# Turning two query tiles of each attention head by VectorE and DRAM instead of one, with every engine's order written for eight units

## What is computed

```python
h = jnp.maximum(_layernorm(x, axis=-1), 0.0)
# layer 2, and layer 3 in the same way with its own weights and biases
q, k, v = split_heads(h @ w_qkv)                       # 8 heads x 1024 x 32
attn = jnp.einsum('bhnd,bhmd->bhnm', q, k) * scale
attn = softmax(where(mask == 0, -inf, attn))
o = jnp.einsum('bhnm,bhmd->bhnd', attn, v)
o = o @ w_proj + b_proj
x = x + o + layernorm(o)                               # layer 2; layer 3: x = x + o
```

## Time and profile before

| | |
|---|---|
| median of three runs | 2766.46 us (2766.36 to 2768.29) |
| the profiled execution's own time | 2763.82 us |
| its span | 2762.0 us |
| busy, share of the span | PE 97%, DVE 81%, ACT 73%, POOL 50% |
| DMA queue of SP | 420192 packets, 364.78 MB, 50.6% of the 16 engines' time |

### The profile page before, as it was taken

The page is one execution under the profiler, slowest core; times in us unless marked ns, Lnnn a source line. Parts: engine busy times, 40 slices in busy tenths (PEclk is TensorE's granted clock), DMA queues, the critical chain, the costliest instruction groups (busy, mean ns, idle before and its releaser), DMA issues.

```text
span 2762.0 us, 59220 instructions
## 1 busy us (share of the span) xinstructions
PE 2679.9 (97%) x22496; PEld 2107.7 (76%) x22496; DVE 2241.6 (81%) x4048; ACT 2022.3 (73%) x3679; POOL 1382.4 (50%) x1600
## 2 busy tenths in 40 slices
PE   9999999899999999999999989999999999999998
PEld 7888888677777777777777767777777777777775
DVE  6767776888888888888888888888888888788876
ACT  3000001888888888888888878888888888888886
POOL 2222221246767676757676758453535353535342
PEclk9999999999999999999999999999999999999999
DMA  3001001756666666665656685756565656566654
GB/s 134 31 31 62 31 31 44 184 148 164 159 161 159 161 159 161 158 161 155 165 151 167 165 212 150 180 141 174 143 175 142 175 136 175 147 166 157 159 138 130
DMA packets 438058, 389.71 MB, mean 141 GB/s; under 512 B 43760, under 2 KB 393968, under 8 KB 437776
## 3 DMA queue, kind: packets, MB, share of 16 engines
q1 hardware_dynamic: 420192, 364.78, 50.6%
q0 software_dynamic: 17584, 21.14, 2.9%
HBM read 139.86 MB, written 94.90 MB: 85 GB/s over the span
## 4 chain that ended last, share of the span: by engine, by line
PE 64%; POOL 7%; DMA 3%; SPq 3%; DVE 2%; issue 2%; ACT 2%; POOLq 0%; ACTq 0%; DVEq 0%
PE t_ring_ps L954 23%; PE t_ot_ps L991 14%; PE t_s_ps L939 14%; PE t_ring_ps L922 5%; PE t_ring_ps L923 4%; PE t_ring_ps L924 4%; POOL t_oT_raw L1577 3%; DMA turned_rows<-t_turned_T 1%; DMA t_R_ot<-inverse_row_sums 1%; SPq L781 1%; POOL t_ot L1559 1%; ACT t_T L1153 1%; PE t_ring_ps L1023 1%; POOL t_xe L1495 1%; DVE t_T L1249 1%
## 5 line engine op out<-in xcount | busy, mean ns | idle before, releaser
L1249 DVE CUSTOM_DVE_ANT_0 t_T<-t_s_ps,mask 128x1024 f32<-128x1024 f32 x1024 | 1226.8, 1212 | 85.1 <-PE t_s_ps L939 79.8
L1153 ACT ACTIVATE t_T<-t_T,t_low 128x1024 f32<-128x1024 f32 x1024 | 1174.1, 1153 | 66.5 <-DVE t_low L1249 64.7
L954 PE MATMUL t_ring_ps<-ident,t_T 128*128 128x128 f32 x7168 | 962.0, 275 | 21.0 <-DVE t_xe L1328 12.7
L954 PEld LDWEIGHTS t_ring_ps<-ident,t_T 128*128 128x128 f32 x7168 | 822.4, 141 | 191.5 <-issue 60.9
L1161 ACT ACTIVATE PT<-t_ring_ps 128x512 f32<-128x512 f32 x1344 | 750.9, 598 | 216.6 <-PE t_ring_ps L954 210.0
L939 PE MATMUL t_s_ps<-t_k,t_q 128*128 128x512 f32 x2048 | 729.1, 437 | 3.5 <-DVE t_low L1249 3.3
L991 PE MATMUL t_ot_ps<-PT,shared 128*32 128x256 f32 x8192 | 498.1, 384 | 13.3 <-DMA PT<-turned_rows 13.3
L991 PEld LDWEIGHTS t_ot_ps<-PT,shared 128*32 128x32 f32 x8192 | 241.8, 110 | 238.5 <-issue 62.9
L1348 DVE COPY PT<-t_ring_ps 128x512 f32<-128x512 f32 x448 | 308.2, 688 | 98.8 <-PE t_ring_ps L954 95.0
L939 PEld LDWEIGHTS t_s_ps<-t_k,t_q 128*128 128x128 f32 x2048 | 309.3, 191 | 46.6 <-DVE t_low L1249 34.3
L273 ACT ACTIVATE g_yT_hi<-g_ps 128x512 fp32r<-128x512 f32 x64 | 38.3, 599 | 379.3 <-PE g_ps L205 379.3
(11 more groups left out here) (170 smaller groups left out, 3889.8 us busy)
## 6 DMA issues: line engine op xcount, KB each, us to landing
turned_rows<-t_turned_T SPq DMA_DIRECT2D x128, 512.0 KB, 3.4
PT<-turned_rows SPq DMA_DIRECT2D x512, 128.0 KB, 2.7
t_q<-t_st_hi SPq DMA_DIRECT2D x256, 128.0 KB, 2.3
t_q<-t_st_lo SPq DMA_DIRECT2D x256, 128.0 KB, 2.4
t_k<-t_st_hi SPq DMA_DIRECT2D x256, 128.0 KB, 2.4
t_k<-t_st_lo SPq DMA_DIRECT2D x256, 128.0 KB, 2.6
t_R_ot<-inverse_row_sums SPq DMA_DIRECT2D x256, 64.0 KB, 2.2
t_oT_raw<-t_ot POOLq DMA_DIRECT2D x512, 32.0 KB, 2.8
```

What stands on the lines that cost most here:

```text
L954: last = nc.tensor.transpose(banks[b][:, i * P:(i + 1) * P], T[u % RING][:, kt * P:(kt + 1) * P], ident[:])
L1153: nc.scalar.activation(T[u % RING][:], T[u % RING][:], ACT.Exp, bias=low[:, u % RING:u % RING + 1], scale=-1.0, accum_out=rsum[:, u:u + 1] ...
L1249: nc.vector.tensor_tensor_reduce(out=T[u % RING][:], in0=s_ps[u % 2][:], in1=mask[:, qt, :], scale=1.0, scalar=3.4e38, op0=ALU.add, op1=AL ...
```

## The change

`FLIPS` becomes (0, 1), so tile 1 of each head takes the way of tile 0, with a second turned_T, a second DRAM tensor and semaphores of its own; room for it comes from w_new, of which two instead of three remain. The layer 3 weights are prepared in job 0 two at a time. `GROUP` becomes 8 and the lists of PE, ACT and DVE are written anew for eight units; the blocks, `BOTH_ON_ACT` (28 units before, 39 after) and `RAW_ON_DVE` (5 before, 7 after) are placed anew. q4 and k4 of a head become one tile, and `load_head` issues six DMAs, of which two carry q and k together. POOL's list has the four MID splits ahead of `turn` 2 and 3. The start of `values` now waits for the copies of the last two units.

```diff
-GROUP = 4
-EARLY = [(1, ("norm", 3)), (11, ("out", 0)), (15, ("out", 1)), (19, ("out", 2)), (26, ("out", 3))]
-MID = [(17, ("qk", 1, 0, 0)), (18, ("norm", 0)), (20, ("qk", 1, 0, 1)), (21, ("qk", 1, 1, 0)),
-       (22, ("qk", 1, 1, 1)), (33, ("norm", 1)), (48, ("norm", 2))]
+GROUP = 8
+EARLY = [(1, ("norm", 3)), (12, ("out", 0)), (17, ("out", 1)), (25, ("out", 2)), (28, ("out", 3))]
+MID = [(18, ("norm", 0)), (19, ("qk", 1, 0, 0)), (20, ("qk", 1, 0, 1)), (21, ("qk", 1, 1, 0)),
+       (22, ("qk", 1, 1, 1)), (33, ("norm", 1)), (49, ("norm", 2))]
-BOTH_ON_ACT = {2, 6, 10, 11, 13, 14, 15, 17, 18, 19, 22, 25, 26, 27, 30, 33, 34, 39, 41, 42, 43, 46, 50, 53, 54, 59, 62, 63}
-RAW_ON_DVE = {20, 34, 37, 49, 52}
-FLIPS = (0,)
+BOTH_ON_ACT = {2, 3, 4, 10, 11, 12, 13, 14, 18, 19, 20, 21, 22, 23, 26, 27, 28, 29, 30, 31, 34, 35, 36, 37, 39, 42, 43, 44, 45, 47, 50, 51, 52, 53, 55, 58, 59, 60, 61}
+RAW_ON_DVE = {20, 22, 34, 36, 38, 50, 51}
+FLIPS = (0, 1,)
...
-                for w, to in enumerate((q4, k4)):
+                for w in range(2):
...
-                    for part in range(4):
-                        dst = slice(part * HD, (part + 1) * HD)
-                        half = (st_hi, st_lo)[part % 2 if w else part // 2]
-                        sp.dma_start(to[s][dst, :].bitcast(F32), half[w][rows, :].bitcast(F32)).then_inc(head_in[s], 16)
+                for part, half in ((0, staged_hi), (3, staged_lo)):
+                    sp.dma_start(qk4[s][part * HD:(part + 1) * HD].bitcast(F32), half[rows].bitcast(F32)).then_inc(head_in[s], 16)
+                for part, halves in ((1, (st_hi, st_lo)), (2, (st_lo, st_hi))):
+                    for w in range(2):
+                        sp.dma_start(qk4[s][part * HD:(part + 1) * HD, w, :].bitcast(F32),
+                                     halves[w][w][rows, :].bitcast(F32)).then_inc(head_in[s], 16)
...
                 for u in range(0, UNITS, GROUP):
                     scores(job, u + 2)
+                    scores(job, u + 3)
                     if u >= NT or before is not None:
-                        for w in range(u, u + GROUP):
+                        for w in range(u, u + 4):
                             values(job, w)
+                    transposes(job, u, 0)
+                    transposes(job, u, 1)
+                    scores(job, u + 4)
+                    transposes(job, u + 1, 0)
                     block_of(u)
...
                     transposes(job, u + 1, 1)
-                    scores(job, u + 4)
-                    block_of(u + 1)
-                    block_of(u + 2)
+                    transposes(job, u + 2, 1)
                     transposes(job, u + 2, 0)
                     scores(job, u + 5)
-                    transposes(job, u + 2, 1)
-                    block_of(u + 3)
                     transposes(job, u + 3, 0)
                     transposes(job, u + 3, 1)
+                    block_of(u + 1)
+                    if u >= NT or before is not None:
+                        for w in range(u + 4, u + 8):
+                            values(job, w)
+                    scores(job, u + 6)
+                    transposes(job, u + 4, 1)
+                    transposes(job, u + 4, 0)
+                    block_of(u + 2)
+                    scores(job, u + 7)
+                    transposes(job, u + 5, 0)
+                    block_of(u + 3)
+                    scores(job, u + 8)
+                    block_of(u + 4)
+                    transposes(job, u + 5, 1)
+                    transposes(job, u + 6, 0)
+                    scores(job, u + 9)
+                    transposes(job, u + 6, 1)
+                    block_of(u + 5)
+                    block_of(u + 6)
+                    transposes(job, u + 7, 0)
+                    transposes(job, u + 7, 1)
+                    block_of(u + 7)
...
                 for u in range(0, UNITS, GROUP):
                     masked(job, u + 2)
+                    masked(job, u + 3)
+                    turn_T(job, u)
                     finish_of(u, ("norm", "out", "v", "qk"))
+                    turn_T(job, u + 1)
+                    masked(job, u + 4)
+                    finish_of(u, ("h",))
+                    finish_of(u + 1, ("h",))
+                    masked(job, u + 5)
+                    finish_of(u + 1, ("norm", "out", "v", "qk"))
...
-                split(job, SPLITS[0])
-                if before is not None:
                     turn(job - 1, 3)
-                split(job, SPLITS[1])
-                split(job, SPLITS[2])
-                split(job, SPLITS[3])
+                    bias_xe(job - 1, before, XE)
```

More of the change, by code:

```diff
@@ L961, in values @@
                 h, kt = u // NT - 1 if u >= NT else HEADS - 1, u % NT
-                if kt == 0:
-                    b, n = place[("T", job, u - 1, 0) if u else ("T", job - 1, UNITS - 1, 0)]
-                    pe.wait_ge(bank_freed[b], n + 1)
-                if kt == HT and job == JOBS:
-                    b, n = place["T", JOBS - 1, UNITS - 1, 1]
-                    pe.wait_ge(bank_freed[b], n + 1)
+                if kt % HT == 0:
+                    j, last = (job, u - kt - 1) if u >= NT else (job - 1, UNITS - 1)
+                    for w in range(last - 1, last + 1):
+                        b, n = place["T", j, w, kt // HT]
+                        pe.wait_ge(bank_freed[b], n + 1)
                 if kt == 0 and h == 0 and job == 0:
@@ new lines, in body @@
+                    finish_of(u + 2, ("norm", "out", "v", "qk"))
+                    masked(job, u + 7)
+                    finish_of(u + 3, ("norm", "out", "v", "qk"))
+                    finish_of(u + 3, ("h",))
+                    finish_of(u + 4, ("h",))
+                    masked(job, u + 8)
+                    if u + 5 not in BOTH_ON_ACT:
+                        copy_pt(job, u + 5)
+                    if u + 6 not in BOTH_ON_ACT:
+                        copy_pt(job, u + 6)
+                    finish_of(u + 4, ("norm", "out", "v", "qk"))
@@ new lines, in body @@
+                    stats_of(u, (0,))
+                    stats_of(u, (1,))
+                    masked(job, u + 9)
+                    if u + 1 not in BOTH_ON_ACT:
+                        copy_pt(job, u + 1)
+                    finish_of(u + 5, ("norm", "out", "v", "qk"))
+                    stats_of(u, (2,))
+                    stats_of(u, (3,))
+                    stats_of(u, (4,))
+                    stats_of(u, (5,))
+                    finish_of(u + 5, ("h",))
+                    stats_of(u, (6,))
@@ new lines, in body @@
+                    finish_of(u + 6, ("norm", "out", "v", "qk"))
+                    finish_of(u + 6, ("h",))
+                    stats_of(u, (7,))
+                    if u + 3 not in BOTH_ON_ACT:
+                        copy_pt(job, u + 3)
+                    if u + 4 not in BOTH_ON_ACT:
+                        copy_pt(job, u + 4)
+                    if u + 7 not in BOTH_ON_ACT:
+                        copy_pt(job, u + 7)
+                    finish_of(u + 7, ("norm", "out", "v", "qk"))
@@ L1407, in body @@
+                    finish_of(u + 7, ("h",))
                     if u not in BOTH_ON_ACT:
                         copy_pt(job, u)
[L1409 to L1416 removed]
@@ L1430, in body @@
                     if job == 0 and u == NT:
                         dve.wait_ge(bias_done, 1)
-                    if job == 0 and NT <= u < NT + 4 * GROUP:
-                        weights_lo((u - NT) // GROUP)
+                    if job == 0 and u in (NT, 2 * NT):
+                        for i in range(2):
+                            weights_lo(2 * (u // NT - 1) + i)
                     if after is not None and u == LN_STEP + NT:
@@ L1616, in body @@
                     add_ln(job - 1, 0)
+                    add_ln(job - 1, 1)
+                for what in SPLITS[0:4]:
+                    split(job, what)
                 if before is not None:
                     turn(job - 1, 2)
-                if before == 0:
-                    add_ln(job - 1, 1)
-                split(job, SPLITS[0])
-                if before is not None:
                     turn(job - 1, 3)
-                split(job, SPLITS[1])
-                split(job, SPLITS[2])
-                split(job, SPLITS[3])
+                    bias_xe(job - 1, before, XE)
                 scale_ot(job, 0)
                 regroup(job, 0)
-                if before is not None:
-                    bias_xe(job - 1, before, XE)
                 if before == 0 and layer == 1:
```

125 lines of the change are left out of this document (66 added, 59 removed).

## The result

The changed kernel takes 2958.95 us (median of four runs, 2953.85 to 2963.78), beside 2766.41 for the kernel before (four runs, 2762.34 to 2768.29): a ratio of 1.070 [1.069, 1.071]. Instead of 61 us faster it is 193 us slower, above the top of the range.

A forecast was written before the change was run, and what follows sets the result against it. PE was taken to bound the attention jobs nearly everywhere, with ACT also full in heads 0, 4 and 7. Gain 5.2 less 1.3 for late tiles, 3.9 us a job, times 16 jobs, 62 us: 2705 us, range 2655 to 2800.

The forecast's parts named there:

- the floor: Attention jobs: larger of PE and ACT busy time per head, 132.3 us; with today's gaps 134.4 or 135.4, 5.2 less.
- the rival of too tight lists: Attention heads: PE, ACT and DVE nearly equally full, each head loses another half microsecond, gain gone: 2769 us; chance 0.19.
- nothing late: Rival for attention jobs: turned tiles land in time, 83 us gained, 2683, or 2641 if block gaps go; chance 0.18.
- DMA occupancy: Attention job: DMA engines' busy time rises from 87 us to 122 of 136, or 0.90; upper-bound tile cost used.
- the rival's d: Turned tiles' write and read chain: delay added by the longer queue; eats the 5.2 us gain at d = 1.2.
- The walk of head 7's tile: SP's queue in head 7: tiles land at 15.1 to 17.1 us, values need them at 14.9; late by 0.2 to 2.2.
- The term "1.0" for head 7: Head 7's turned tiles: assumed lateness of 1.0 us a job, taken from a range of 0.2 to 2.2.
- The term "0.3" for head 3: Head 3's turned tiles: assumed lateness of 0.3 us a job, landing at 16.3 to 18.3 against 17.1.
- The long heads 1, 2, 5 and 6 have three and more: DRAM way in heads 1, 2, 5 and 6: turned tiles have three us or more to spare, so no loss.
- The rival of late tiles: Heads 7, 3, 0, 4: longer queue makes every turned tile late; 8.3 us a job at d = 2, 2816; chance 0.20.
- above 100, the late tiles won: Sign: PE's wait at L991 for turned rows, 13.3 us before, expected 15 to 40; above 100 means late tiles.
- median landing below 4: Sign at L781, the turned tile's landing: its median should be below 4 if the forecast holds.

The follow-up runs named there:

- e2: Changed kernel with tile 1's write to DRAM, read back and PE's wait for it left out (computes another result): 2713.44 us, ratio 0.981.
- f4: Kernel before, old lists kept, with tile 1 also turned by DVE and moved through DRAM in heads 2, 5 and 6: 2816.99 us, ratio 1.018.
- e8: Changed kernel with head 1's load of the next x issued after the turned tiles' reads instead of ahead of them: 2854.46 us, ratio 1.032.
- e9: Changed kernel with tile 1 moved and awaited only in heads 2, 4, 5 and 6 (computes another result): 2726.02 us, ratio 0.986.
- e11: Changed kernel with x loaded after head 1's reads and tile 1 not moved in heads 3 and 7 (computes another result): 2743.53 us, ratio 0.992.

## Why the prediction was wrong

**PE, ACT, DVE and the floor: right.** By heads PE was to be busy 13.7, 14.7, 20.6, 15.9, 15.3, 18.8, 18.8, 13.3; the medians of e2's stretches are 15.3, 15.1, 20.5, 16.0, 16.7, 19.1, 18.8, 14.2. The turns end at 5.5 us into the groups of heads 3 and 7 where 5.6 was said, ACT is full in head 7 (in head 0, where it was also to have no gap, it is busy for 13.73 of 15.9 us in e2's job 4), and exp waits for DVE less than before (39.2 us instead of 64.7). They add to 135.7, for a forecast job of 134.4 or 135.4 with nothing late. The largest excess is head 4, 16.7 for 15.3, so of the rival of too tight lists perhaps 1 us a job is true. e2 saves 53 us and not the 83 of "nothing late", since a job of it is 4.4 shorter than before instead of 5.2 (70 us), and the first tile is late in some jobs.

**DMA occupancy: right as a number, wrong in its use.** 122 us a job were forecast; share times length in the rows of job 4 gives 124. That the mean would be near 0.9 was called the real unknown, and then went into no term of the sum but the rival's d. In the traces the fuller queue goes with two costs. Writes land at 4.7 us in the middle instead of 3.4, and reads at 3.1 instead of 2.7. SP itself takes longer to issue: 4.51 us for eight reads in head 7, 8.63 in head 1, where 0.45 each was taken. The share of a head alone doesn't say where that hurts: heads 7 and 1, whose tiles are late, have 0.88 and 0.94, but so is the tile of head 3 at 0.73, and the tiles of head 4 are in time at 0.98.

**The walk of head 7's tile: 3.6 us too short, the first step that failed.** Forecast, in the middle: load done at 5.9, moves, write and half of the reads in 7.5, landing 2.7, at 16.1. Measured in job 4: load done at 8.1, moves and first write 4.4, eight reads 4.5, at 17.1, then 2.65 to land, 19.7. The load was done 2.2 later (it began at 2.5 where 1.7 was said, and its six issues took 5.6 us, 0.51 to 1.15 each, where 0.6 to 0.8 was said), and the first tile's reads didn't fit ahead of the second write's landing as the text assumed (1.5). PE was ready at 16.2 and waited 3.55. The term "1.0" for head 7 is 3.6 us of waiting and 1.3 of lower clock, and the job's stretch of head 0 is 4.9 longer in the median than in e2 (20.2 - 15.3). The term "0.3" for head 3 is 4.2 (20.9 - 16.7). Of the job's loss, 1.3 us were put down to these two, and they cost 9.1.

**Head 1: the second step that failed.** "The long heads 1, 2, 5 and 6 have three and more." By the prediction's own sum head 1 is no long head any more: it loses an output block and its transposes and comes to 14.7. And the load of x, 1 MB between its moves and its reads, was not on the walk at all, though SP's list passes it. Head 2 therefore waits 5.6 us in job 4 and is 7.6 longer than in e2, the largest loss of all, at a place where the text had no term, and moving x takes it away.

**The clock: no term.** Neither the forecast nor its rivals price a slow stretch behind a wait. The rival of late tiles summed only waits: 4d + 0.3. With d at the 1.7 by which the two medians rose it gives 7.1 us a job, 1.9 more than the gain, 2797. It took the right mechanism, the right side and the right place of decision (d above 1.2), and "above 100, the late tiles won" was the right reading beforehand; it missed head 1, and the 85 us, a third of the 241, by which PE's busy time grew over e2 with the same instructions, at a mean granted clock of 0.954 for 0.990.

The Trainium skill's sentence on HBM, 0.2 us on average and 2 us at high load ("DMA: Bandwidth & Descriptors", Latency and other measured facts), was weighed and given the smaller chance since the median of the earlier trace rows hadn't moved. The trace after agrees with its direction: +1.3 on a write, +0.4 on a read. By its size in series, 2 x 1.8 us, the rival gives 4 x 3.6 + 0.3 = 14.7 us a job and 2918, an estimate nearer to the result than any in the prediction, but by luck: the landings rose by 1.7 together and not by 3.6, and neither head 1 nor the clock is in it. The criterion "median landing below 4" was useless: it is 3.1 in a kernel 193 us slower, since the few reads that PE waits for don't show in the median of 1024.

## What to carry to other kernels

When work moves from a full engine to DMA, walk every tile of every head through the issuing queue with the occupancy of the new kernel, and list what stands between its write and its read; a transfer that nobody waits for soon (here x) goes behind those that somebody does. Walk on past the head that gets the extra tile: what stands behind it in the list moves back too (f4). Recompute which stretches are long after the change, before you call one safe. Price a wait of the matmul engine as the wait and the slow stretch that may follow it.

## What was not expected of the hardware

The time to issue isn't a constant of the DMA: eight equal reads took 3.81 us on SP (head 3), 4.51, 5.62 (e8) and 8.63, the last behind a 1 MB load. After a wait of 2.47 us, in head 4, the granted clock of the next 3.6 us was 0.53, and after one of 5.63 us 0.64; a wait of 3.21 us in the same trace was followed by values at full speed, 1.93 us. And the bytes of tile 1 cost 13 us when moved in four heads (e9 over e2) and 111 in two others (e8 over e11).
